# A chain of layers on one core: norm, operands and attention as one stage, the mixture fused with its norms, and PV for two key tiles in one go

## The chip, the cores and the metric

The kernel runs on one core of a Trainium2 chip. The metric is the device time of one execution in microseconds (us). Engines: TensorE (PE: matmuls, PEld: weight loads), VectorE (DVE), ScalarE (ACT), GpSimd (POOL) and SyncE (SP), which here issues nearly all DMAs.

## The reference

On 8 batches of 512 tokens by 128 channels in float32, the reference runs four layers, each an attention part and a feed-forward part, with a norm, a residual and another norm around every part. What the change touches:

- L0 attention: 16 heads of 8 channels. Its heads are a reshape of the token axis and not a split of the channels, so that a head's rows are gathered from many tokens. `softmax(Q K^T) V`, plus x, and a variance over a whole batch.
- L3 attention: 16 heads of 8 channels, rotary embedding on q and k, biases, `softmax(Q K^T / sqrt(8)) V`, output projection.
- L3 feed-forward: an elastic mixture of 4 experts (128 to 512 to 128, ReLU), each weighted per token by a gate value u (a sigmoid) and a rule on u; then the last norm and residual, which is the output.
- The norm: `(x - mean) / sqrt(var + 1e-5)` over 128 channels.

Between them lie channel mix, a test-time learner, a switch layer, linear attention and expert choice, which stay as they are.

## The kernel before

The program is a list of stages (`program`, L2355 on). Each opens a block in which every engine gets its own instruction list; engines meet only by semaphores, and all of them meet at a stage's end. Tokens lie as 32 tiles of 128 tokens by 128 channels; a batch is 4 tiles (`TPB`).

`norms` (L148) is one stage for all 8 batches: VectorE takes statistics (L183, L186), POOL makes scale and shift of a tile (L257 to L260), ScalarE applies them (L344), VectorE adds the residual (L223), TensorE transposes the normalised tiles (L332) and VectorE copies them to `c.nT` (L227). There are nine such stages, norm0 to norm8.

`attention_operands` (L417) is the next stage. For each batch it projects q and k (L486; with rotary also a swapped version, L488) and v (L493), and splits q and k into three bfloat16 parts, so that nine products of bfloat16 rows give a float32-like score: first part on ScalarE (L511), remainder on VectorE (L558), second part on ScalarE (L501), third part on POOL (L601); POOL adds the rotated halves (L590). SP stores the parts in device memory (L462) and loads them in the layout of a quad (L401, L403). VectorE lays v out (L576, L580).

`attention` (L604) runs over 32 quads. A quad is 4 heads' groups of 512 queries and 512 keys. For quad i the kernel needs the maxima of its scores first: 8 max tiles of two matmuls each (L731) into two pairs of banks, reduced by VectorE (L881); POOL splits the maxima in three (L691 to L697), TensorE transposes them (L744), ScalarE copies them (L854), and SP moves them (L662) into the operand rows, so that the score matmul (L750) subtracts the maximum. Then for each of 4 key tiles k there are 4 score matmuls g, an exponential each (L850) and PV for the key tile (L760: 4 column groups of the array, float32). In steady state the maxima of quads i+2 and i+3 are made beside the scores of quad i. TensorE's list, in a loop of four quads, is: score g=0, score g=1, PV of the key tile before, score g=2, a max tile, score g=3, a max tile. Scores have two banks in turn, probabilities two sets. After a quad VectorE copies the output (L890 for L0, L892 for L3). L0 regroups rows on POOL (L409); L3 selects rows by small matmuls (L771). VectorE normalises (L899, L901, L908, L910).

`elastic_mixture` (L2145) prepares the gate's weights for all tokens, loads w1 and w2, and in a second block runs 32 steps (batch by expert): 4 up matmuls (L2208), ReLU (L2242), 16 down matmuls (L2215), and VectorE gathers the weighted result (L2273). The gate's matmuls (L319) are in norm7, the output's store (L362) in norm8.

Of the kernel before, what the change touches and what calls it, by code (L numbers as in the profile page):

```python
# [4 lines left out]
F32 = mybir.dt.float32  # L5
# [367 lines left out]
class Attention:  # L373
# [5 lines left out]
    def __init__(self, c, tag, by_tokens, scale):  # L379
        self.c, self.tag, self.by_tokens, self.scale = c, tag, by_tokens, scale  # L380
        nc = c.nc

        self.q_parts = nc.dram_tensor(f"{tag}_q_parts", (B, PARTS, TPB, HD, 2048), BF16).ap()
        self.k_parts = nc.dram_tensor(f"{tag}_k_parts", (B, PARTS, TPB, HD, 2048), BF16).ap()

        self.q9 = c.take(RING * 1024).bitcast(BF16).rearrange("p (s t) -> p s t", s=RING)
        self.k9 = c.take(RING * 1024).bitcast(BF16).rearrange("p (s t) -> p s t", s=RING)
        if by_tokens:
            self.q_raw = c.take(RING * 1024).rearrange("p (s t) -> p s t", s=RING)
            self.k_raw = c.take(RING * 1024).rearrange("p (s t) -> p s t", s=RING)  # L390
        self.v32 = c.take(2 * 512).rearrange("p (s g k d) -> p s g k d", s=2, g=4, k=4)
        self.qk_in = [c.sem(f"{tag}_qk_in{s}") for s in range(RING)]

        self.v = c.take(QUADS * 128).rearrange("p (q g k d) -> p q g k d", g=4, k=4, d=HD)

    def load(self, sp, b, s):

        q_to, k_to = (self.q_raw.bitcast(BF16), self.k_raw.bitcast(BF16)) if self.by_tokens else (self.q9, self.k9)
        for p in range(PARTS):
            src = self.q_parts[bass.ds(b, 1), p, s].rearrange("o d t -> (o d) t")  # L400
            sp.dma_start(q_to[24 * p:24 * p + 24, s, :],  # L401
                         src.unsqueeze(0).to_broadcast([PARTS, HD, 2048])).then_inc(self.qk_in[s], 16)
            sp.dma_start(k_to[24 * p:24 * p + 24, s, :],  # L403
                         self.k_parts[bass.ds(b, 1), :, s].rearrange("o r d t -> (o r) d t")).then_inc(self.qk_in[s], 16)

    def by_group(self, pool, n, s, signal):

        for raw, rows in ((self.q_raw, self.q9), (self.k_raw, self.k9)):
            pool.tensor_copy(rows[0:QK_ROWS, s, :].bitcast(F32).rearrange("p (g j l) -> p g j l", g=4, j=HEADS),  # L409
                             raw[0:QK_ROWS, s, :].rearrange("p (j g l) -> p g j l", g=4, j=HEADS)).then_inc(signal, 1)  # L410

    def columns(self, rows, g, first, n):

        return rows[:, 512 * g + first:512 * g + first + n]


def attention_operands(c, a, w, tables=None):  # L417

    nc = c.nc
    tag = a.tag + "_op"
    sem = lambda name: c.sem(f"{tag}_{name}")
    q_made, v_made = sem("qk_made"), sem("v_made")
    high, rest, mid, parts, v_laid = (sem(s) for s in ("high", "rest", "mid", "parts", "v_laid"))
    SLOTS = 4
    stored = [sem(f"stored{s}") for s in range(SLOTS)]
    exact = sem("exact")
    LOAD_AT = SLOTS - 1  # L430
    part = c.take(SLOTS * PARTS * 256).bitcast(BF16).rearrange("p (s a t) -> p s a t", s=SLOTS, a=PARTS)
    left = c.take(SLOTS * S).rearrange("p (s t) -> p s t", s=SLOTS)
    if tables is not None:
        full = c.take(SLOTS * S).rearrange("p (s t) -> p s t", s=SLOTS)
        turn = c.take(SLOTS * S).rearrange("p (s t) -> p s t", s=SLOTS)

# [1963 lines left out]
```

## Time and profile before

| | |
|---|---|
| median of 3 runs | 2471.12 us (2436.83, 2471.12, 2471.49) |
| profiled execution | 2424.76 us |
| its span, first to last instruction | 2423.0 us |
| granted TensorE clock, mean | 0.800 |
| busy: PE, DVE, ACT, POOL | 69%, 57%, 46%, 27% |
| instructions | 30093 |

Busy shares are means over stages that differ much. A trace row gives start and length in us, engine, line of the kernel and operation, out<-in with shapes, and in brackets how long the engine had been idle and what ended that. The granted clock is the share of TensorE's full clock.

### The profile page before, as it was taken

To read this page: it belongs to the slowest core of one execution; us is meant where nothing else is said; L and a number is where in the kernel's file an instruction comes from. 1 tells how busy PE (TensorE), PEld (TensorE's weight loads), DVE (VectorE), ACT (ScalarE), POOL (GpSimd) and SP (SyncE) were. 2 spreads that over 40 slices of the span, in tenths; PEclk is the share of its full clock that TensorE was granted. 3 is DMA by queue.
4 is the path that set the end of the run, shared out by engine and by line. 5 is a ranking of instruction groups with operands and counts; after the bars stand their busy time and mean duration, and the time that the engine had idled before them with its cause. 6 is when DMAs were issued, how large, how long until landed. Compare 5 with 4: busy or idle time off the path is not lost. (4 is left out here: it accounts for less than half of the span.)

```text
span 2423.0 us, 30093 instructions
## 1 busy us (share of the span) xinstructions
PE 1679.4 (69%) x8625; PEld 859.8 (35%) x8625; DVE 1376.5 (57%) x3051; ACT 1121.6 (46%) x2093; POOL 651.0 (27%) x1168
## 2 busy tenths in 40 slices
PE   3389999992469952605530185346999999759995
PEld 2212222221346642503430164121333333347774
DVE  4578888865822462034468711646778787453334
ACT  4237777774431241216640031423777777553343
POOL 3222222215510035161051875542000000040002
PEclk9779999995756965756755588576999999959997
DMA  3311111100000003100004022121111111010001
GB/s 80 117 34 50 50 48 48 47 17 0 1 1 1 1 1 101 33 20 1 0 5 135 4 43 26 42 98 42 48 46 44 49 44 46 2 35 0 0 0 35
DMA packets 84907, 84.54 MB, mean 35 GB/s; under 512 B 35927, under 2 KB 67522, under 8 KB 84694
## 3 DMA queue, kind: packets, MB, share of 16 engines
q1 hardware_dynamic: 74902, 76.43, 9.5%
q0 software_dynamic: 7680, 6.06, 1.5%
q10 hardware_dynamic: 2240, 1.05, 0.2%
q8 instruction: 36, 0.59, 0.1%
q14 instruction: 49, 0.40, 0.1%
HBM read 59.78 MB, written 25.17 MB: 35 GB/s over the span
## 5 line engine op out<-in xcount | busy, mean ns | idle before, releaser
L881 DVE TENSOR_REDUCE arena<-psum 128x2 f32<-128x1024 f32 x512 | 603.2, 1219 | 148.6 <-PE psum L731 145.6
L850 ACT ACTIVATE arena<-psum 128x512 f32<-128x512 f32 x1024 | 581.7, 596 | 202.3 <-PE psum L750 180.5
L750 PE MATMUL psum<-arena 99*128 99x512 bf16 x1024 | 390.4, 389 | 20.0 <-ACT arena L850 8.6
L731 PE MATMUL psum<-arena 72*128 72x512 bf16 x1024 | 322.1, 397 | 30.7 <-PEq L448 13.1
L344 ACT ACTIVATE arena<-arena 128x128 f32<-128x128 f32 x512 | 208.4, 481 | 219.9 <-POOL arena L260 194.5
L760 PE MATMUL psum<-arena 128*32 128x512 f32 x2048 | 275.4, 610 | 1.9 <-ACT arena L850 1.9
L332 PE MATMUL psum<-arena 128*128 128x128 f32 x256 | 71.2, 433 | 271.5 <-ACT arena L344 271.5
L750 PEld LDWEIGHTS psum<-arena 99*128 99x128 bf16 x1024 | 98.2, 99 | 403.2 <-ACT arena L850 338.1
L257 POOL TENSOR_SCALAR arena<-arena 128x4 f32<-128x4 f32 x104 | 26.3, 253 | 650.3 <-DVE arena L186 642.7
L691 POOL TENSOR_TENSOR arena<-arena 128x16 bf16<-128x16 f32 x64 | 13.9, 217 | 671.6 <-DVE arena L881 420.1
L183 DVE BATCH_NORM_STATS2 arena<-arena 128x6 f32<-128x128 f32 x512 | 110.3, 278 | 86.9 <-DMA arena<-sw_rows_out,arena 33.7
L2242 ACT ACTIVATE arena<-psum,arena 128x512 f32<-128x512 f32 x128 | 88.1, 689 | 139.9 <-PE psum L2208 139.4
L731 PEld LDWEIGHTS psum<-arena 72*128 72x128 bf16 x1024 | 99.7, 100 | 143.3 <-DVE arena L881 23.5
L332 PEld LDWEIGHTS psum<-arena 128*128 128x128 f32 x256 | 47.5, 223 | 289.4 <-ACT arena L344 289.4
L259 POOL TENSOR_TENSOR arena<-arena 128x4 f32<-128x4 f32 x120 | 128.6, 1072 | 10.4 <-DVE arena L191 1.6
L2215 PEld LDWEIGHTS psum<-arena 128*128 128x128 f32 x1024 | 119.1, 191 | 14.9 <-issue 14.9
L2208 PE MATMUL psum<-arena 128*128 (+1 forms) x256 | 116.6, 599 | 9.8 <-ACTq L2235 9.8
L2273 DVE SCALAR_TENSOR_TENSOR arena<-psum,arena 128x128 f32 (+1 forms) x128 | 36.0, 344 | 152.1 <-PE psum L2215 137.9
L2215 PE MATMUL psum<-arena 128*128 128x128 f32 x1024 | 119.3, 274 | 0.0
L486 PE MATMUL psum<-arena 128*128 128x512 f32 x64 | 44.8, 813 | 79.9 <-DVE arena L558 41.1
L2026 ACT ACTIVATE arena<-psum,arena 128x512 f32<-128x512 f32 x8 | 6.2, 777 | 172.7 <-PE psum L1986 172.7
L1197 ACT ACTIVATE arena<-psum 128x512 f32<-128x512 f32 x48 | 28.7, 598 | 120.7 <-PE psum L1135 63.8
(374 smaller groups left out, 2493.8 us busy)
## 6 DMA issues: line engine op xcount, KB each, us to landing
arena<-L_q_parts SPq DMA_DIRECT2D x192, 96.0 KB
arena<-L_k_parts SPq DMA_DIRECT2D x192, 96.0 KB
L_q_parts<-arena SPq DMA_DIRECT2D x16, 384.0 KB, 3.2
L_k_parts<-arena SPq DMA_DIRECT2D x16, 384.0 KB, 3.2
arena<-in_L_ffn_w SPq DMA_DIRECT2D x1, 2048.0 KB, 10.5
ec_result<-arena SPq DMA_DIRECT2D x1, 2048.0 KB, 9.8
arena<-in_L_ffn_fc2s SPq DMA_DIRECT2D x1, 2048.0 KB, 16.3
ec_normed<-arena SPq DMA_DIRECT2D x1, 2048.0 KB, 8.7
```

The source lines that it names most:

```text
L183: nc.vector.bn_stats(f.stats[:, t, :], src[:, t, :]).then_inc(s_stats, 1)
L259: ch.next(nc.gpsimd.tensor_tensor(f.scale[:, at], f.var_eps[:, at], c.minus_half[:, 0:n], ALU.pow))
L332: last = nc.tensor.transpose(c.bank(b % 2)[:, k * 128:(k + 1) * 128], c.n[:, TPB * b + k, :], c.ident)
L344: nc.scalar.activation(dst[:, t, :], src[:, t, :], ACT.Identity, bias=f.shift[:, t:t + 1], scale=f.scale[:, t:t + 1]).then_inc(signal, 1)
L731: last = nc.tensor.matmul(max_bank[m % 2][:, 512 * h:512 * h + 512], a.columns(q9[0:QK_ROWS, s, :], m // 2, 128 * (2 * (m % 2) + h), 128), ...
L750: nc.tensor.matmul(score_bank[g % 2], a.columns(k9[0:ROWS, s, :], g, 128 * k, 128), a.columns(q9[0:ROWS, s, :], g, 0, 512), start=True, st ...
L760: last = nc.tensor.matmul(out_bank[32 * g:32 * g + 32, :], v32[:, s % 2, g, k, :], prob[:, k % 2, g, :], start=(k == 0), stop=(k == 3))
L850: nc.scalar.activation(prob[:, k % 2, g, :], score_bank[g % 2], ACT.Exp, scale=a.scale).then_inc(probs, 1)
L881: nc.vector.tensor_reduce(neg_max[:, s % 2, col:col + 2], max_bank[m % 2].rearrange("p (h t) -> p h t", h=2), axis=AX.X, op=ALU.max, negat ...
L2208: nc.tensor.matmul(c.bank(k), w1[:, e, 128 * k:128 * k + 128], batch, start=True, stop=True).then_inc(h_made, 1)
L2215: last = nc.tensor.matmul(c.bank(4 + e % 2)[:, 128 * t:128 * t + 128], hT[:, e % 2, k, 128 * t:128 * t + 128], w2[:, e, k, :], start=(k == ...
L2242: nc.scalar.activation(hT[:, e % 2, k, :], c.bank(k), ACT.Relu, bias=b1T[:, CHUNKS * e + k:CHUNKS * e + k + 1]).then_inc(h_done, 1)
```

## The change

It has four parts.

1. **One stage per attention.** `attention_layer` takes the place of norm0, `attention_operands` and `attention` of L0, and of norm6, operands and attention of L3. Before the first quad only batches 0 and 1 are normalised, projected and stored. Batch b+2 is handled beside the four quads of batch b: ScalarE applies the norm tile by tile between exponentials, TensorE transposes and projects behind the max tiles of certain key tiles, ScalarE copies the results out of PSUM, and POOL does all the splitting of operands, the rotary products and the laying out of v (of batches 0 and 1 VectorE splits q). All loops are written out.
2. **One ring of three banks for ScalarE** (banks 4, 5, 7). Scores, row transposes, token transposes and projections take its slots in a fixed order. Maxima and, for L3, the selection use the two pairs of banks in turn as a second ring.
3. **PV for two key tiles in one go, three probability sets.** PV of key tiles 0 and 1 comes after the second score of key tile 2, PV of 2 and 3 after the second score of the next quad's key tile 0.
4. **Mixture fused.** norm7, mixture and norm8 are one stage: the norm, gate and weights of batch b+1 are made beside the steps of batch b, and the last norm and store of batch b-1 too. `project_heads` now follows a barrier of its own.

The diff's core (the rest follows from it: removed are `Attention`, `attention_operands`, `attention`; waits are on constants now):

```
+    def beside(i, k):
+        kind = {(1, 2): "n", (1, 3): "q", (2, 3): "k", (3, 3): "v"}.get((i % TPB, k))
+        b = i // TPB + AHEAD                      # AHEAD = 2
+        return items(b)[kind] if kind and b < B else ()
+    acts = Ring([c.bank(4), c.bank(5), c.bank(7)], for_scalar())
+    maxes = Ring([c.bank(0, 2), c.bank(2, 2)], for_vector())
+    def split_parts(eng, ch, b, n):
+        a, f = part[:, slot_of(b, n), :, :], full[:, n, :]
+        if rope:
+            ch.mark(eng.tensor_tensor(f, f, cos_t, ALU.mult))
+            ch.next(eng.tensor_tensor(other[:, n, :], other[:, n, :], sin_t, ALU.mult))
+            ch.next(eng.tensor_tensor(f, f, other[:, n, :], ALU.add))
+        ch.next(eng.tensor_copy(a[:, 0, :], f))
+        ch.next(eng.tensor_tensor(f, f, a[:, 0, :], ALU.subtract))
+        ch.next(eng.tensor_copy(a[:, 1, :], f))
+        eng.tensor_tensor(a[:, 2, :], f, a[:, 1, :], ALU.subtract).then_inc(part_done[n], 1)
...
+        SP:  for i in range(QUADS):
+                if i < LAST:
+                    max_rows(i + 1)
+                b = i // TPB + AHEAD
+                if i % TPB >= 2 and b < B:
+                    store(b, i % TPB - 2)
+                if by_tokens and i + 5 < QUADS:
+                    load(i + 5)
+                if rope and i + RING < QUADS:
+                    load(i + RING)
...
+        POOL: for i in range(QUADS):
+                r, b = i % TPB, i // TPB + AHEAD
+                if i < LAST:
+                    values(i + 1)
+                if r == 0 and b < B:
+                    of_x.factors(pool, b)
+                if r == 0 and AHEAD < b <= B:
+                    lay_values(b - 1)
+                if rope and r == 1 and b + 1 < B:
+                    of_o.factors(pool, b + 1)
+                if r >= 2 and b < B:
+                    operand(b, r - 2)
+                if by_tokens and i + RING < QUADS:
+                    regroup(i + RING)
+                if i + 2 < QUADS:
+                    split_max(i + 2)
...
+        TensorE, quad i, key tile k:
+                    if k == 0:
+                        pe.wait_ge(max_in[i % RING], 16 * (i // RING + 1))
+                    score_tile(i, k, 0)
+                    score_tile(i, k, 1)
+                    if k == 2:
+                        pv(i, 0)
+                        pv(i, 1)
+                    if k == 0 and i >= 1:
+                        pv(i - 1, 2)
+                        pv(i - 1, 3)
+                    score_tile(i, k, 2)
+                    score_tile(i, k, 3)
+                    if rope and k == 1 and i >= 1:
+                        pick(i - 1)
+                    if i + 2 < QUADS:
+                        if k == 0:
+                            operands_set(i + 2)
+                        max_tile(i + 2, 2 * k)
+                        max_tile(i + 2, 2 * k + 1)
+                    if k == 1 and i < LAST:
+                        turn_max(i + 1)
+                    (batch b: turn_tokens at (1, 2), queries at (1, 3), keys at (2, 3), project_values at (3, 3))
...
+        ScalarE, at = 4 * (i % TPB) + k, after exps(i, k):
+                    if k == 1 and i < LAST:
+                        rows(i + 1)
+                    if b < B and 1 <= at <= 4:
+                        of_x.apply_tile(act, c.n, c.x, TPB * b + at - 1)
+                    if rope and b + 1 < B and 5 <= at <= 8:
+                        of_o.apply_tile(act, c.o, c.o, TPB * b + at - 1)
+                    (copy_tokens at 6, keep q at 7, keep k at 11, keep_values at 15)
...
+        VectorE, quad i, key tile k:
+                    if k == 0 and i >= 1:
+                        out(i - 1)
+                    if k == 1 and i >= 1:
+                        normalise(i - 1)
+                    if i + 2 < QUADS:
+                        take(i + 2, 2 * k)
+                        take(i + 2, 2 * k + 1)
+                    (o_spread at (0, 2), add at (2, 2), x_spread at (3, 2))
...
+        Mixture, TensorE:
+            for g in range(STEPS):
+                b, e = divmod(g, MIX)
+                if g + 1 < STEPS:
+                    up(g + 1)
+                if b + 1 < B and e == 2:
+                    turn(b + 1)
+                if b + 1 < B and e == 3:
+                    gate(b + 1)
+                down(g)
...
-        stage(norms, "norm0", after_layer=False)
...
-        stage(norms, "norm6", after_layer=True, reload=chosen_sums)
-        stage(rotary_attention, d, rotary)
-        stage(norms, "norm7", after_layer=True, gate=mixture.wu)
-        stage(elastic_mixture, d, mixture)
-        stage(norms, "norm8", after_layer=True, x_norm=False, out=out)
+        stage(rotary_attention, d, rotary, chosen_sums)
+        stage(elastic_mixture, d, mixture, out)
```

The lines in words ("SP:", brackets) are for orientation and not in the code.

## Rows read from the trace of the kernel before

**Rows 1.** The page, busy time, share of the span and instructions of each engine.
```profile
PE 1679.4 (69%) x8625; PEld 859.8 (35%) x8625; DVE 1376.5 (57%) x3051; ACT 1121.6 (46%) x2093; POOL 651.0 (27%) x1168
```

**Rows 2.** Stretches: start:end, length, busy of PE, PEld, DVE, ACT, POOL; clock.
```profile
21.70:148.50 126.80, 57.45 (x163) 26.30 (x163) 83.67 (x235) 38.85 (x66) 44.28 (x63) 0.75 0.24 69
129.00:147.00 18.00, 15.48 (x32) 2.28 (x33) 16.63 (x15) 0.27 (x1) 7.15 (x12) 0.50 0.00 1
148.50:552.00 403.50, 390.38 (x2046) 109.43 (x2045) 320.39 (x338) 296.23 (x543) 91.14 (x212) 0.99 0.11 42
214.55:264.49 49.94, 49.24 (x261) 14.04 (x260) 42.18 (x44) 37.16 (x68) 12.50 (x28) 1.00 0.13 48
1519.10:1675.40 156.30, 72.01 (x195) 30.91 (x195) 92.14 (x251) 53.41 (x99) 73.14 (x105) 0.64 0.19 66
1675.40:2100.40 425.00, 413.48 (x2301) 139.16 (x2301) 318.66 (x336) 296.26 (x544) 33.88 (x154) 0.98 0.11 40
1851.67:1904.23 52.56, 51.83 (x293) 17.69 (x292) 42.13 (x45) 37.17 (x68) 4.41 (x20) 1.00 0.12 46
2114.40:2169.80 55.40, 20.89 (x97) 20.07 (x97) 30.68 (x148) 27.99 (x67) 29.76 (x64) 0.53 0.12 38
2169.80:2396.00 226.20, 225.98 (x1280) 163.44 (x1280) 70.76 (x261) 88.14 (x128) 0.00 (x0) 0.99 0.00 0
2396.00:2423.00 27.00, 0.00 (x0) 0.00 (x0) 15.88 (x76) 13.18 (x32) 16.69 (x32) 0.54 0.27 78
```

**Rows 3.** Timeline of one key tile in an L0 quad.
```profile
308.55 2.39 ACT L850 ACTIVATE arena<-psum 128x512 f32<-128x512 f32 x4 [0.66 <-PE psum L750]
309.44 0.81 PE L750 MATMUL psum<-arena 99*128 99x512 bf16 x2
310.18 1.06 PE L760 MATMUL psum<-arena 128*32 128x512 f32 x8
311.18 0.39 PE L750 MATMUL psum<-arena 99*128 99x512 bf16 x1
311.60 2.39 ACT L850 ACTIVATE arena<-psum 128x512 f32<-128x512 f32 x4 [0.66 <-PE psum L750]
312.04 2.36 DVE L881 TENSOR_REDUCE arena<-psum 128x2 f32<-128x1024 f32 x2 [0.51 <-PE psum L731]
```

**Rows 4.** Timeline, selecting matmuls of an L3 quad and the load behind them.
```profile
1856.09 1.08 PEld L771 LDWEIGHTS psum<-arena 128*128 128x128 f32 x8
...
1857.00 0.21 PEld L750 LDWEIGHTS psum<-arena 99*128 99x128 bf16 x2
```

**Rows 5.** Timeline, project_heads: four transposes, four matmuls, the next transposes.
```profile
2108.30 0.60 PE L2089 MATMUL psum<-arena 128*128 128x128 f32 x4
...
2108.74 1.06 PE L2100 MATMUL psum<-arena 128*128 128x128 f32 x8
...
2109.63 0.60 PE L2089 MATMUL psum<-arena 128*128 128x128 f32 x4
```

**Rows 6.** Timeline and DMA issues, pieces of the serial stretches.
```profile
21.74 0.87 DVE L183 BATCH_NORM_STATS2 arena<-arena 128x6 f32<-128x128 f32 x4 [21.74 <-PEq L100]
...
25.10 1.65 ACT L344 ACTIVATE arena<-arena 128x128 f32<-128x128 f32 x4 [3.83 <-POOL arena L260]
...
65.58 0.70 SPq L401 DMA_DIRECT2D arena<-L_q_parts  x1
...
1568.44 0.69 DVE L558 TENSOR_TENSOR arena<-arena 128x512 f32<-128x512 f32 x1
1568.47 1.79 POOL L590 TENSOR_TENSOR arena<-arena 128x512 f32<-128x512 f32 x1 [0.73 <-DVE arena L548]
...
1571.52 1.09 POOL L601 TENSOR_TENSOR arena<-arena 128x512 bf16<-128x512 f32 x1 [1.26 <-ACT arena L501]
...
1572.56 3.47 DVE L568 MEMSET arena<- 32x4096 int32 x1 [0.91 <-issue]
...
1575.04 7.03 ACT L515 ACTIVATE arena<-arena 32x8192 bf16<-32x8192 f32 x1
...
L_q_parts<-arena SPq DMA_DIRECT2D x16, 384.0 KB, 3.2
```

More of the change, by code:

```diff
@@ L370 @@
 RING = 4
[L373 to L414, printed above, removed]
@@ L417, in attention_operands, with __init__, bank, count @@
-def attention_operands(c, a, w, tables=None):
+class Ring:
+    def __init__(self, banks, names):
+        self.banks = banks
+        self.number = {name: n for n, name in enumerate(names)}
+    def bank(self, name):
+        return self.banks[self.number[name] % len(self.banks)]
+    def count(self, name):
+        return self.number[name] + 1
+    def room(self, name):
+        return max(0, self.number[name] + 1 - len(self.banks))
+AHEAD = 2
+def attention_layer(c, tag, w, scale, tables=None, reload=None):
@@ L474, in _, with turn_tokens, project @@
         @block.tensor
         def _(pe):
+            def turn_tokens(b):
+                pe.wait_ge(of_x.normed, TPB * (b + 1))
+                pe.wait_ge(act_taken, acts.room(("n", b)))
+                for k in range(TPB):
+                    last = nc.tensor.transpose(acts.bank(("n", b))[:, 128 * k:128 * k + 128], c.n[:, TPB * b + k, :], c.ident)
+                last.then_inc(act_made, 1)
+            def project(name, weights):
+                b = name[1]
+                pe.wait_ge(act_taken, max(acts.count(("n", b)), acts.room(name)))
+                nc.tensor.matmul(acts.bank(name), weights, c.nT[:, b, 1:S + 1], start=True, stop=True).then_inc(act_made, 1)
@@ new lines, in pv @@
+            def pv(i, k):
+                pe.wait_ge(act_taken, acts.count(("score", i, k, 3)))
+                if k == 0:
+                    pe.wait_ge(v_ready, i + 1)
+                    pe.wait_ge(out_taken, i)
+                for g in range(4):
+                    last = nc.tensor.matmul(out_bank[32 * g:32 * g + 32, :], v32[:, i % 2, g, k, :],
+                                            prob[:, (4 * i + k) % PROBS, g, :], start=(k == 0), stop=(k == 3))
+                last.then_inc(pv_step, 1)
@@ L476, in _, with pick @@
+            def pick(i):
+                pe.wait_ge(out_taken, i + 1)
+                pe.wait_ge(max_taken, maxes.room(("pick", i)))
+                for t in range(4):
+                    last = nc.tensor.matmul(maxes.bank(("pick", i))[:, 36 * t:36 * t + 36], o_quad[:, i % 2, 128 * t:128 * t + 128],
+                                            select, start=True, stop=True)
+                last.then_inc(max_made, 1)
             pe.wait_ge(ordered, 1)
@@ L2150, in elastic_mixture @@
+def elastic_mixture(c, d, small, out):
     nc = c.nc
```

1100 lines of the change are left out of this document (600 added, 500 removed).

## The prediction

> **What bounds the kernel now.** I read the engines' totals first, then the time by stretches, then the order of work inside one quad. The totals [rows 1] name no bound: TensorE 69%, VectorE 57%, ScalarE 46%. The stretches [rows 2] show why. The attention quads run with TensorE recorded as almost always busy, at full clock, VectorE at 84% and ScalarE at 74% (49.94 us for four quads of L0, 12.49 each; 52.56 for four of L3, 13.14 each). Ahead of each attention lies a serial stretch, 126.8 us for L0 and 156.3 us for L3, in which no engine reaches 70% and no exponential runs: norm of all batches, operands of all batches, first maxima. At the end, 55.4 us of norm and preparation lead to the mixture's 226.2 us, which TensorE fills (225.98 busy), and 27.0 us of last norm follow, with TensorE idle.
>
> Inside a quad neither TensorE nor ScalarE is the bound alone: the wait that ends last is a loop [rows 3]. ScalarE does four exponentials in 2.39 us, then idles 0.66. The second of them (end at 308.55 plus 1.20) is the last of a key tile. It frees the bank of a score that starts 0.1 later, PV of the finished tile follows 0.33 behind (310.18) and takes 1.0, the next score starts at 311.18 and reaches ScalarE 0.42 later (311.60). So the loop is 1.20 + 0.43 + 1.0 + 0.42 = 3.05 us per key tile: with two banks and two probability sets, what ScalarE still has in store is shorter than PV and its two handovers. Four of them and the 0.27 us row copy are 12.47, against 12.49 measured. L3 adds the four small selecting matmuls, which hold TensorE 0.91 us [rows 4], of which 0.65 shows.
>
> **The change part by part.** All sums are against the profiled execution, 2424.76 us (span 2423.0).
>
> *Start of L0.* After the change only two batches precede the first quad. Norm of one batch ends 5.0 us after its start (25.10 plus 1.65 less 21.74) [rows 6]; transposing, copying and projecting q at half clock bring the first operand to about +10. VectorE meanwhile has three statistics of 1.25, the pad memset of 3.47 and the ones memset. The ones memset stood on ScalarE at 7.03; VectorE's price for it is unseen: 3.5 if it goes by bytes as the pad memset, 7 if by elements; I take 7. So VectorE starts its operand at +15; four operations of 0.7 with three handovers of 0.16 end at +18. The store is issued and lands 3.2 to 3.7 later, six loads are issued at 0.74 each (0.70 and a gap) and land as much later: +30 [rows 6]. Regrouping takes 2 us, sixteen maxima at 1.18 [rows 3] go to +51, and the first score needs all but the last two: first exponential at about +50 where it is now +126.8. Gain 76.5.
>
> *Start of L3.* Two norms with the residual between give +10.7, four projections at half clock (1.8 each, twice the 0.89 of [rows 5]) and their copies +21. VectorE, with spreads, adds and memsets, is free at +24; seven operations on it take 5.7: +30. Store, loads and maxima as before: first exponential at +60 for 156.3 now. Gain 96. Bound for both starts: 10 us either way each.
>
> *A quad.* I follow the new order from the first score after a PV pair (t=0). Scores 0 and 0.21, two maxima tiles to 1.28, the four scores of the next key tile to 2.6, two maxima tiles, of which the second waits until VectorE, behind the output copy (0.7), has read the earlier one (3.5); the row transpose; scores of the third key tile at 4.09 and 4.3, the latter after the second tile's last exponential; then PV twice, 1.9. The score behind it starts at 6.42 and its exponential at 6.84, though ScalarE had finished at 5.75: 1.1 us idle. The second half is alike, with one exponential fewer in the chain because no transpose takes a bank, but the last maxima tile waits for VectorE until 9.9 and the two scores and the PV pair end at 12.68. So the loop now has 11 exponentials (6.6), two PV pairs (3.8), two pairs of scores (0.86), two round trips (1.04) and 0.4 of VectorE's lateness. The third bank and third set let the first PV of a pair start without a wait, but nothing hides the second one. For L0: 12.68 for 12.49, over 32 quads +6. For L3 the selection moves into VectorE's ring of two banks: the max tile behind it waits until the normalising (0.25, 0.17, 0.29) is done, at about 4.66, so 13.84 for 13.14: +22. Bounds: the engines' own sums. For L0 VectorE has 8x1.18 and 1.5, 11.0; for L3 TensorE has 32 matmuls of 0.213, four PV of 0.95, 0.16 and 0.91, 11.7.
>
> *Side work for six later batches.* TensorE takes four transposes (0.44) and projections (0.89 each) [rows 5]: three for L0 (3.1 us), five for L3 (4.9 us). They stand in TensorE's queue between maxima and scores, so I count them whole. ScalarE's copies behind the second and fourth key tiles fall into its idle time after a PV pair; those behind the first and third (0.41 each) show partly, 0.2. VectorE's statistics behind the maxima delay the output copy by 0.7 (L0), 1.3 with the second norm (L3). Batch sums 3.9 and 6.4; times six: +23.5 and +38. POOL has 16 small copies, operands and regrouping, some 31 us of L0's 50 per batch, in L3 less than 30: nothing waits for it. If that cover goes, each late operand delays a store, and the row transfer behind it on SP. First-quad transpose wait +2, no PV pair in the first quad -1.9, in either layer.
>
> *Mixture.* The norm and residual of batch 0 only, then transposes, copy and gate: first up matmul 14.6 after the start, for 55.4 now. The 226.2 stay; seven further batches add 0.44 and 0.86 each on TensorE, +9. ScalarE and VectorE have room in a batch of 28 us (88.14 and 70.76 busy in 226.2). Behind the last down: 1.2, one norm 5.0, residual 0.7, store 2.7: 9.6 for 27.0. From 308.6 to 259.4: -49.
>
> Sum: L0 -76.5+6+23.5 = -47. L3 -96+22+38 = -36. Mixture -49. One more barrier +1. In all -131: 2294 for the profiled execution.
>
> A side remark on POOL. One of its two-input operations took 1.79 us beside VectorE's two-input operation instead of 1.09 to 1.3 [rows 6]. At the starts, VectorE and POOL split operands at once; at 0.5 for each of some 16 meetings, of which half lie on the path, that is +4, inside the bounds. The Trainium skill (SBUF — State Buffer, Who interferes with whom) says that a VectorE instruction with two inputs in SBUF shares a read port with GpSimd and that one fully blocks. By that rule alone all 16 VectorE operations of 0.69 would be added, 11 us, and the sum would be 2305. The quads are free of it: VectorE's maxima read PSUM.
>
> **The rivals.**
>
> *More is hidden* (0.20). Side work falls into existing waits and the loop is shorter than I traced. For it: ScalarE would still be idle 2.8 of 12.68. Against it: the same method reproduces today's 12.49 to 0.02. The floor is 371 us for L0's quads and 403 for L3's, where I have 435 and 485: 2148; halfway to it, 2220.
>
> *A queue is late* (0.23). SP issues six loads (4.4 us) and, before some, waits for a store; the max-row transfer of the next quad stands behind them. For it: today's row transfers have fewer waits ahead. Against it: the loads are freed about 9 us into a quad, the rows are wanted only 4 us into the next. At 1 us a quad it is 2358, at 2 us 2422, which would be no change.
>
> *The clock* (0.05, slower). With TensorE recorded busy for 15.48 of 18.0 us in the first maxima, the clock was 0.50 [rows 2]; in the quads it is 1.00. That is 1.2 and 2.4 GHz. If PV pairs and waits leave TensorE idle enough for the lower level, a quad costs twice 10.8 instead of 12.68, +9 for L0, and twice 11.7 instead of 13.84, +9.6 for L3. The kernel is slower by over 2% from 19 of the 64 quads on (180 us at 9.3 each); 20 of them give 2480 on the profiled scale. Against it: TensorE's own work per quad is 85% of the time, hardly less than now (87%).
>
> **How the numbers follow.** The forecast case has the remaining 0.52. The three timed runs lie 12, 46 and 47 us above the profiled execution; I add 21, near 1%, for where a median will lie: 2315. The forecast's own range is 2265 to 2355 (starts 10 each, k-ones and port 10, side work 20, offset 20). For 8 in 10 I reach into the first two rivals: 2210 to 2400. A change under 2% is hardly told from none here. Faster by over 2% (profiled time under 2376): the forecast, the first rival and half of the second, 0.83. Within 2%: 0.12. Slower: 0.05.
>
> **What would show it.** First exponentials 50 and 60 us behind the stages' first VectorE instruction (now 126.8 and 156.3); output copies 12.7 and 13.8 apart in late quads and about 1 to 1.6 more in the earlier ones; ScalarE idle about 1.1 us twice a quad, released by TensorE; the mixture's steps 7.0 us as now, and under 12 us behind the last. Wrong would be: quads under 12 us, first scores waiting for the row transfer, POOL named as releaser of scores, or a granted clock under 0.9 in the quads.

## Result: 2328 us for 2457, and where the terms landed

The changed kernel takes 2328.3 us as the median of four runs (2302.2 to 2356.0), the kernel before 2457.5 (four runs). Two of the four runs took 2302 and 2304 us at a mean granted clock of 0.82, two 2353 and 2356 us at 0.80, and the ratio, 0.938 (95% interval 0.923 to 0.952), compares the shorter runs of either kernel: faster, near the forecast of 2315 and inside the range. The profiled execution took 2302.2 us (span 2300.5), where my sum said 2294. The page's totals for the changed kernel, in the columns of [rows 1]:

```profile
PE 1619.6 (70%) x8625; PEld 838.0 (36%) x8625; DVE 1307.5 (57%) x2847; ACT 1072.9 (47%) x2122; POOL 789.8 (34%) x1434
```

As before they name no bound. The stretches do. The changed kernel's, in the columns of [rows 2]: start of L0, its quads, the learner's stage with the norm ahead of it, expert choice, start of L3, its quads, and the fused mixture to the end:

```profile
20.95:83.31 62.36, 26.20 (x67) 8.07 (x68) 38.71 (x52) 8.01 (x18) 27.99 (x46) 0.67 0.20 66
83.30:514.90 431.60, 396.25 (x2142) 123.06 (x2140) 324.33 (x374) 297.60 (x591) 176.56 (x397) 0.99 0.15 51
602.40:822.30 219.90, 163.94 (x801) 111.74 (x802) 95.38 (x332) 70.76 (x147) 29.75 (x64) 0.76 0.00 1
1203.00:1453.20 250.20, 110.16 (x759) 79.67 (x759) 124.37 (x269) 31.16 (x44) 133.08 (x161) 0.67 0.22 50
1477.31:1550.30 72.99, 34.40 (x75) 11.30 (x76) 51.68 (x93) 17.12 (x35) 35.83 (x58) 0.57 0.22 75
1550.30:2022.70 472.40, 439.35 (x2414) 157.95 (x2412) 332.53 (x419) 313.45 (x623) 142.57 (x298) 0.97 0.13 47
2040.89:2300.40 259.51, 238.65 (x1377) 174.98 (x1377) 112.92 (x496) 129.42 (x242) 44.50 (x96) 0.96 0.06 17
```

The kernel before, the two stretches whose code the change leaves alone (same columns):

```profile
638.30:878.90 240.60, 185.57 (x802) 124.48 (x802) 95.72 (x332) 70.80 (x147) 29.77 (x64) 0.68 0.00 1
1259.60:1491.00 231.40, 104.62 (x759) 75.77 (x759) 124.21 (x270) 31.28 (x44) 129.17 (x159) 0.68 0.23 53
```

Set against the forecast, in us ("copies": from the first to the last copy of a quad's output, 31 intervals):

| stretch | before | forecast | after |
|---|---|---|---|
| L0, first VectorE instruction to first exponential | 126.8 | 50 | 62.4 |
| L0 copies | 385.2 | 414.7 | 412.3 |
| L3, the same start | 156.3 | 60 | 73.0 |
| L3 copies | 404.0 | 464 | 454.9 |
| last norm, mixture, last norm | 308.6 | 259.4 | 259.5 |
| learner's stage (code unchanged) | 240.6 | 240.6 | 219.9 |
| expert choice (code unchanged) | 231.4 | 231.4 | 250.2 |

The starts came out 25 us worse than forecast, L3's quads 9 better, and two stages that the change doesn't touch moved by -20.7 and +18.8, which happen to cancel. (Expert choice is counted to VectorE's last instruction here. From its start to the first instruction of the next stage it is 274.3 us for 259.5, +14.8.) The differences in the table sum to -120.7, the spans differ by 122.5.

Half an L0 quad of the changed kernel without side work, as a timeline (start, length; in brackets the idle time before it and what ended it; answers to [rows 3]):

```profile
455.76 1.08 ACT L840 ACTIVATE arena<-psum 128x512 f32<-128x512 f32 x2 [1.25 <-PE psum L734]
455.78 1.03 PE L721 MATMUL psum<-arena 72*128 72x512 bf16 x4
456.64 0.82 PE L734 MATMUL psum<-arena 99*128 99x512 bf16 x3
457.12 2.07 ACT L840 ACTIVATE arena<-psum 128x512 f32<-128x512 f32 x4 [0.28 <-PE psum L734]
457.78 0.39 PE L734 MATMUL psum<-arena 99*128 99x512 bf16 x1 [0.31 <-ACT arena L840]
458.00 0.60 PE L721 MATMUL psum<-arena 72*128 72x512 bf16 x2
458.83 0.60 PE L721 MATMUL psum<-arena 72*128 72x512 bf16 x2 [0.23 <-DVE arena L925]
459.53 0.61 PE L734 MATMUL psum<-arena 99*128 99x512 bf16 x2
460.02 1.08 ACT L840 ACTIVATE arena<-psum 128x512 f32<-128x512 f32 x2
460.07 1.93 PE L744 MATMUL psum<-arena 128*32 128x512 f32 x16
461.93 0.61 PE L734 MATMUL psum<-arena 99*128 99x512 bf16 x2
462.35 1.09 ACT L840 ACTIVATE arena<-psum 128x512 f32<-128x512 f32 x2 [1.25 <-PE psum L734]
```

L734 is the score, L840 the exponential, L721 the maxima, L744 PV. While TensorE does the pair of PVs (460.07 to 461.93), ScalarE runs dry: 1.25 us idle, and as much half a quad before. Four exponentials in a row take 2.07 us when their scores are ready, not the 2.39 of [rows 3], so ScalarE is not what the loop is made of. TensorE stands for others in the key tile behind each pair: 0.31 for a bank that ScalarE has not emptied, 0.23 for maxima that VectorE has not taken. Twice a quad this makes 1.08 us, all that TensorE's record lacks (11.83 busy of 12.91). What I had traced as one loop is two engines that wait for each other in turn.

### The profile page after: what moved, and what is told of

The parts are those of the page before. It is cut to its first block and busy times, and to the rows that moved or that the text cites. A ratio compares the mean times of both kernels' runs of the same rounds, so it can differ in the third digit from the quotient of the medians.

```text
span 2300.5 us, 26232 instructions
## 1 busy us (share of the span) xinstructions
PE 1619.6 (70%) x8625; PEld 838.0 (36%) x8625; DVE 1307.5 (57%) x2847; ACT 1072.9 (47%) x2122; POOL 789.8 (34%) x1434
## 5 line engine op out<-in xcount | busy, mean ns | idle before, releaser
L840 ACT ACTIVATE arena<-psum 128x512 f32<-128x512 f32 x1024 | 540.3, 601 | 213.3 <-PE psum L734 208.5
L734 PE MATMUL psum<-arena 99*128 99x512 bf16 x1024 | 318.5, 390 | 54.2 <-ACT arena L840 36.2
L721 PE MATMUL psum<-arena 72*128 72x512 bf16 x1024 | 301.3, 399 | 58.8 <-DVE arena L925 20.7
L744 PE MATMUL psum<-arena 128*32 128x512 f32 x2048 | 256.7, 619 | 0.2
L734 PEld LDWEIGHTS psum<-arena 99*128 99x128 bf16 x1024 | 84.8, 98 | 308.1 <-ACT arena L840 219.1
L344 ACT ACTIVATE arena<-arena 128x128 f32<-128x128 f32 x320 | 129.4, 481 | 127.0 <-POOL arena L260 101.6
L332 PE MATMUL psum<-arena 128*128 128x128 f32 x160 | 44.5, 433 | 172.9 <-ACT arena L344 172.9
L721 PEld LDWEIGHTS psum<-arena 72*128 72x128 bf16 x1024 | 88.2, 99 | 209.0 <-DVE arena L925 80.1
L623 POOL COPY arena<-arena 72x1024 f32<-72x1024 f32 x64 | 65.0, 1042 | 180.9 <-PE psum L734 157.7
L2330 PEld LDWEIGHTS psum<-arena 128*128 128x128 f32 x1024 | 118.1, 192 | 8.2 <-issue 8.2
L2330 PE MATMUL psum<-arena 128*128 128x128 f32 x1024 | 119.9, 275 | 0.0
L257 POOL TENSOR_SCALAR arena<-arena 128x4 f32<-128x4 f32 x56 | 14.2, 254 | 303.2 <-DVE arena L186 299.2
L2318 PE MATMUL psum<-arena 128*128 128x512 f32 x256 | 116.9, 600 | 0.0
L2451 DVE SCALAR_TENSOR_TENSOR arena<-psum,arena 128x128 f32<-128x128 f32 x128 | 36.0, 344 | 127.1 <-PE psum L2330 126.4
L744 PEld LDWEIGHTS psum<-arena 128*32 128x32 f32 x2048 | 54.2, 111 | 136.2 <-issue 89.9
L332 PEld LDWEIGHTS psum<-arena 128*128 128x128 f32 x160 | 29.7, 224 | 183.7 <-ACT arena L344 183.7
L2253 ACT ACTIVATE arena<-arena 128x128 f32<-128x128 f32 x124 | 50.3, 481 | 92.7 <-POOL arena L2241 92.7
```

What stands on the lines that cost most here:

```text
L332: last = nc.tensor.transpose(c.bank(b % 2)[:, k * 128:(k + 1) * 128], c.n[:, TPB * b + k, :], c.ident)
L344: nc.scalar.activation(dst[:, t, :], src[:, t, :], ACT.Identity, bias=f.shift[:, t:t + 1], scale=f.scale[:, t:t + 1]).then_inc(signal, 1)
L623: nc.gpsimd.tensor_copy(rows[0:QK_ROWS, i % RING, :].rearrange("p (g j l) -> p g j l", g=4, j=HEADS), raw[0:QK_ROWS, i % RAW, :].rearrange ...
L721: last = nc.tensor.matmul(bank[:, 512 * h:512 * h + 512], columns(q9[0:QK_ROWS], i, m // 2, 128 * (2 * (m % 2) + h), 128), columns(k9[0:QK ...
L734: nc.tensor.matmul(acts.bank(name), columns(k9[0:ROWS], i, g, 128 * k, 128), columns(q9[0:ROWS], i, g, 0, 512), start=True, stop=True).the ...
L744: last = nc.tensor.matmul(out_bank[32 * g:32 * g + 32, :], v32[:, i % 2, g, k, :], prob[:, (4 * i + k) % PROBS, g, :], start=(k == 0), sto ...
```

## Experiments

All spans of stretches below are from one profiled execution each.

**The fused mixture alone** on the kernel before: its last three stages replaced by

```
-        stage(norms, "norm7", after_layer=True, gate=mixture.wu)
-        stage(elastic_mixture, d, mixture)
-        stage(norms, "norm8", after_layer=True, x_norm=False, out=out)
+        stage(elastic_mixture, d, mixture, out)
```

> Edit: the kernel before with the changed kernel's mixture alone (LayerNorm inside it, steps unrolled, output stored batch by batch); norms, operands and attention stay as separate stages. By the prediction's term the tail from the last attention stage on goes from 308.6 to 259.4 us, so the whole is 49 us shorter than before: a ratio of 0.980. Rival A: the first start of the mixture depends on what the attention stage leaves (queues, banks), so that the gain differs from the changed kernel's own 259.6 us by more than 2 us. Rival B: part of the 49 us was a gain of the joint stage, and the ratio is 0.987 or above (under 32 us). The mixture's 32 steps should stand 7.0 us apart.

Ratio to before 0.980 (0.971 to 0.989). From the last output copy of L3 to the end: 325.0 us before, 276.9 here, 277.8 in the changed kernel. So -48.1 of the forecast -49, by itself, within 1 us of the changed kernel: by this stretch both rivals fall. The whole can't decide: its interval reaches past the 0.987 at which rival B begins, and the profiled span is only 3.3 us shorter than before, because two stages of unchanged code took longer, the learner's 271.2 us for 240.6 and expert choice some 14 more. Four steps of the mixture, one batch, take 29.4 us for 28.0, the 1.3 of the batch's own transposes and gate on TensorE.

**PV for one key tile at a time**, on the changed kernel:

```
-                    if k == 2:
-                        pv(i, 0)
-                        pv(i, 1)
+                    if k >= 1:
+                        pv(i, k - 1)
                     if k == 0 and i >= 1:
-                        pv(i - 1, 2)
                         pv(i - 1, 3)
```

> Edit: the changed kernel with PV for one key tile at a time (after the scores 0 and 1 of the next key tile), three probability sets kept. Theory: the quad is TensorE's own list plus two short waits per key tile (for the fourth score's bank and for the second half of the maxima); each lone PV of 0.93 us stands between the scores, so ScalarE has a stall of about 0.4 us in each key tile instead of 1.25 us in every second, and the sum of TensorE's list is unchanged: late quads of layer 0 within 0.2 us of the changed kernel's 12.91, those of layer 3 within 0.2 of 13.75, whole within 10 us. Rival A (the diff's second half is what costs: two PV in a row drain the score ring): late quads 12.5 in layer 0, near the kernel before's 12.49, the whole 20 to 25 us shorter. Rival B (two PV at once save a wait each): 13.3 or more, the whole 20 us longer.

Late quads: 11.63 us in L0, 12.86 in L3. My theory fell, and rival A was too timid: the copies span 375.9 us in L0 and 423.7 in L3, 36.4 and 31.3 less than the changed kernel. Three windows: a late quad of the changed kernel,

```profile
455.47:468.38 12.91, 11.83 (x66) 3.48 (x65) 10.41 (x11) 8.75 (x17) 3.18 (x8) 1.00 0.04 16
```

and, with PV split, a late quad and 100 us of earlier ones:

```profile
424.00:435.63 11.63, 11.63 (x73) 3.44 (x65) 10.36 (x12) 8.97 (x19) 3.21 (x7) 1.00 0.04 14
350.00:450.00 100.00, 100.00 (x561) 30.92 (x563) 87.45 (x95) 76.94 (x148) 35.55 (x82) 1.00 0.14 48
```

In L0 TensorE's record has no pause left. Its timeline with PV split shows why: ScalarE's pauses are short and even, and TensorE has no wait in brackets:

```profile
431.73 0.60 PE L734 MATMUL psum<-arena 99*128 99x512 bf16 x2
432.21 1.09 ACT L837 ACTIVATE arena<-psum 128x512 f32<-128x512 f32 x2 [0.28 <-PE psum L734]
432.26 1.06 PE L744 MATMUL psum<-arena 128*32 128x512 f32 x8
433.26 0.61 PE L734 MATMUL psum<-arena 99*128 99x512 bf16 x2
433.69 1.09 ACT L837 ACTIVATE arena<-psum 128x512 f32<-128x512 f32 x2 [0.39 <-PE psum L734]
433.71 1.03 PE L721 MATMUL psum<-arena 72*128 72x512 bf16 x4
```

So PV in pairs, part 3 of the change, costs 68 us in the two layers. Some 8 of L3's 31 are a matter of the clock. Five of the changed kernel's 31 intervals between L3's copies are 1.6 us longer than their like. In each, about 5 us behind the copy, the granted clock fell to 0.5 (1.2 GHz) for 3.4 us and a PV pair took 3.1 to 3.6 us for 1.92. One such stretch with its clock, its pair, and the same pair of a quad earlier:

```profile
1618.50:1621.90 3.40, 3.40 (x18) 0.60 (x16) 1.40 (x2) 1.38 (x4) 0.00 (x0) 0.50 0.05 14
1618.80 3.46 PE L744 MATMUL psum<-arena 128*32 128x512 f32 x16
1604.06 1.92 PE L744 MATMUL psum<-arena 128*32 128x512 f32 x16
```

Ahead of each fall TensorE had stood for the bank and the maxima (0.31 and 0.23 us). The two other profiles with the changed kernel's quads show five such falls each, those with interleaved maxima and without side work one each. The kernel before and all seven kernels with PV split show none between L3's copies. Why these five of 31, and none in L0, stays open.

Yet the whole (median 2283.6, ratio 0.938) was only 8 us shorter in the profiled execution: the learner's stage, same code, took 282.7 us for 219.9. More on that below.

**Maxima interleaved**, on the changed kernel: scores 0, 1, (PV), 2, maxima a, score 3, maxima b.

> Edit: the changed kernel with TensorE's order in a key tile changed from scores 0, 1, 2, 3, maxima a, b to scores 0, 1, 2, maxima a, score 3, maxima b. Theory (TensorE's list with its two short waits sets the quad): the first maxima fill the wait of 0.31 to 0.5 us for score 3's bank, and VectorE begins on them earlier, so that the second wait (0.23 to 0.39) shrinks too: late quads of layer 0 12.0 to 12.3 us instead of 12.91, layer 3 12.9 to 13.2 instead of 13.75; 62 quads by 0.6 to 0.9 make 35 to 55 us less in all. Rival A (the loop through ScalarE's exponentials sets it): score 3 comes 0.3 to 0.4 us later to ScalarE in every key tile, and quads are 13.0 to 13.6, the whole 10 to 40 us longer. Rival B (VectorE's two reductions per key tile set it): no change, quads within 0.1 us of 12.91.

Late quads 12.47 and 13.16; copies 399.2 and 432.0 us, 13 and 23 less. The direction is the theory's, the size half of it in L0: the wait for the bank went, the one for the maxima stayed, at 0.30 twice a quad. The whole (median 2327.6 us, ratio 0.957, 0.950 to 0.964) would have misled: its profiled execution took 2327.3 us, 25 more than the changed kernel's, and again the learner's stage took 282.6.

**The first row of maxima ahead of the loads of quad 3**:

```
             load(2)
-            load(3)
             max_rows(0)
+            load(3)
```

> Edit: at the start of each attention stage of the changed kernel the transfer of the first quad's row of maxima is issued on SyncE's queue before the loads of quad 3 instead of behind them. Theory: that 12 KB transfer landed 8 to 10.5 us after its issue since it stood behind the loads of quads 2 and 3; with one of them behind it, it lands in 4 to 7 us, and the first exponential is 3 to 6 us earlier in each layer, 6 to 12 us in all. Rival A: a row transfer takes as long in any place (a scattered write), no change within 2 us. Rival B: SyncE waits for the row's own source and holds the loads of quad 3 back, so that quad 3's operands are late: first exponential earlier but the third or fourth quad longer by as much, the sum unchanged.

L3's start in the changed kernel, with the row's transfer (SPq L549) and the first score and exponential:

```profile
1538.69 0.74 SPq L549 DMA_DIRECT2D arena<-arena  x1
1549.65 1.91 PE L734 MATMUL psum<-arena 99*128 99x512 bf16 x4 [6.82 <-DMA arena<-arena]
1550.29 2.07 ACT L840 ACTIVATE arena<-psum 128x512 f32<-128x512 f32 x4 [10.33 <-PE psum L734]
```

and with the row first:

```profile
1542.13 0.74 SPq L549 DMA_DIRECT2D arena<-arena  x1
1546.07 1.93 PE L734 MATMUL psum<-arena 99*128 99x512 bf16 x4
```

11.0 us from issue to score become 3.9. The theory holds for L3: the first exponential comes 65.7 us after the stage's first VectorE instruction, 71.7 to 73.7 in seven profiles with the row behind the loads. L0 shows rival B: the first exponential is 4.6 us earlier (78.72 for 83.31), the first copy 3.7 later (106.24 for 102.57), for TensorE's transpose for quad 1 then waits for POOL, which waits for quad 3's late operands, regroups them (2.0 us) and lays out values (5.5 us) ahead of splitting quad 1's maxima:

```profile
94.41 0.30 PE L728 MATMUL psum<-arena 128*48 128x128 bf16 x1 [9.28 <-POOLq L636]
```

The Trainium skill (DMA: Bandwidth & Descriptors, Queues, rings and completion order) says that a queue's descriptors on one DMA engine are consumed in ring order. These runs agree: from the issue of a 12 KB transfer to the score that needs it are 11.0 us, or 3.9 and perhaps less for the landing, by what stands ahead of it.

**No side work in the quads**: norm, projections and operands of batches 2 to 7 left out, and those of the first two read again.

> Edit: the changed kernel without the work of the later batches inside the quads (norm, transposes, projections, operands, stores of batches 2 to 7; for L3 of batches 2 to 7 as well); the quads of the later batches read the operands of the first two again. It leaves that part of the computation out. Theory of the prediction: the side work cost 3.9 us (layer 0) and 6.4 us (layer 3) for each of six batches, and nothing else slows the early quads: all quads of layer 0 at the late quads' 12.91 us, of layer 3 at 13.75; from first to last output copy 412.3 becomes 395 us in layer 0 (six times 2.87 less), 454.9 becomes 418 in layer 3 (six times 6.2 less). Rival A: late quads are short since the loads have ended too, so that quads without side work but with loads are 13.2 or more. Rival B: the POOL's share of the side work only stands at an idle place, and early quads stay within 0.3 us of what they were.

Up to the last two, which have no maxima beside them, every quad of L0 is 12.91 (copies 395.1 us) and every one of L3 13.75 (421.3), but for one of 15.44 in which the clock fell. So side work costs 17.2 us in L0, 2.87 for each of six batches. In L3 33.6 us went with it, but four falls of the clock, some 6.6 us, are part of that, which leaves 27, 4.5 a batch. The loads are hidden, as the theory has it.

**Two banks in ScalarE's ring**, with PV split: `acts = Ring([c.bank(4), c.bank(5)], for_scalar())`.

> Edit: PV for one key tile at a time, as in the run with PV split (late quads 11.63 and 12.86 us), and ScalarE's ring of two banks in place of three. Theory: with three banks and lone PVs TensorE was busy without a pause (100.00 us of 100); with two banks the third score waits for the first exponential in each key tile, some 0.2 to 0.4 us, four times a quad: late quads of layer 0 12.3 to 12.9 us, near the kernel before's 12.49, which had two score banks and lone PVs as well. Rival A: TensorE's list hides these waits, quads within 0.1 us of 11.63, and the third bank is worth nothing. Rival B: transposes, side projections and the scores share two banks now, and early quads rise by over 1.5 us while late ones don't.

Late quads 11.98 and 13.21, 0.35 more only; quads with side work 13.5 to 14.2 in L0 where they had been 12.5. Copies 403.9 and 451.0: the third bank is worth 28 and 27 us, nearly all of it where side projections share the ring. Rival B in kind, not the theory: of its 1.5 us for early quads, 0.9 to 1.7 came for three in four and 0.4 for the fourth.

**Two probability sets**, with PV split: `PROBS = 2`.

> Edit: PV for one key tile at a time and two probability sets in place of three. Theory: a lone PV of key tile k-1 ends before the exponentials of k+1 begin, so that two sets do: quads within 0.1 us of 11.63 in layer 0 and 12.86 in layer 3. Rival: the exponentials of k+1 wait for the PV of k-1, which stands behind two scores, and the quad is 0.4 to 1.2 us longer (up to 12.8).

Copies 375.9 and 423.6, late quads 11.63 and 12.86: no difference at all. The third set buys only the pairing, which costs.

**The best version**: PV split, in L3 alone the row first, and

```
-            nc.vector.memset(k9[MAX_ROW:128, :, :], 1.0).then_inc(k_ones, 1)
+            nc.vector.memset(k_words[MAX_ROW:128, :, :].rearrange("p s t -> p (s t)").bitcast(I32), 0x3F803F80).then_inc(k_ones, 1)
```

> Edit: the changed kernel with PV for one key tile at a time; in layer 3 the first row of maxima issued before the loads of quad 3; and the ones of the key operands written as 32-bit words (half as many elements). Theory: against the changed kernel's profiled run 36 us less in layer 0's quads, 31 in layer 3's (as in the run with PV split), 7.5 at layer 3's start, 3.4 at each start from the ones, some 81 us in all if the stages between, whose code is the same, take what they took there (2220 us); with the learner's stage at the lower granted clock, as in the run with PV split (283 instead of 220 us), 2210 to 2285. Ratio to the kernel before 0.91 to 0.935. Rival A: the ones are hidden behind the loads, and both starts stay (7 us more). Rival B: the learner's stage is at the lower clock in all runs of this kernel, because layer 0's quads leave TensorE no pause: no run below 2265. Rival C: it comes and goes from run to run whatever stands before it: the runs fall into groups 20 to 60 us apart, the lowest below 2240.

Median 2254.9 us (2238.7 to 2263.6, six runs); ratio to before 0.933 (0.922 to 0.943). The ones take 3.47 us for 6.88. L0's first exponential comes 59.4 us after the stage's first VectorE instruction, 62.4 to 62.9 in the seven profiles without these ones and without the row first. L3's comes after 65.1, for 65.7 with the row first alone, and after 63.6 to 64.7 in three later profiles: there the ones give 2 us at most, so that rival A is partly right. Copies 376.0 and 423.7. The learner's stage took 266.6 us. All six runs lie within 25 us, below rival B's 2265 and in no two groups as rival C has it. Against the changed kernel's first profile the span is 48 us shorter: the stretches that were edited gave some 78, the learner's stage took 47 back, and expert choice, code unchanged, gave 15. The Trainium skill (VectorE: DVE Perf Modes, Zero memsets can be issued as uint32) says that a memset takes one cycle per element whatever the type: the 6.88 and 3.47 agree, and here for a value other than zero.

**The changed kernel again**, beside the next three:

> The changed kernel once more, beside the next three, to have its stages of unchanged code against theirs. Theory (the granted clock of the learner's stage differs from run to run whatever stands before it): layer 0 412.3 and layer 3 454.9 us from first to last output copy, as in its first profile, and the learner's stage anywhere between 220 and 283 us. Rival (the joint stage with its pauses leaves the learner a higher clock): the learner's stage within 5 us of 220 again and its fast runs at 2295 to 2305.

Copies 412.2 and 454.9; learner's stage 222.2 us; runs 2287.9 to 2290.6, and one of 2362.9; ratio 0.940 (0.931 to 0.949). The rival's 220 within 5, the shorter runs 5 to 7 us below its 2295. The run of 2362.9, at a granted clock of 0.79 for 0.82, was not profiled, so that the theory doesn't fall either. Expert choice took 231.1 us, for 250.2 in this kernel's first profile.

**Idle time before the learner**, on the best version: a stage of nine VectorE memsets after its norm, between 605.5 and 644.1 us.

> Edit: the best kernel so far (PV split, layer 3's row first, 32-bit ones) with a stage of nine VectorE memsets, some 38 us in which TensorE does nothing, put in before the learner's stage. It took 2252.6 us with the learner's stage at 266.6 us, where the changed kernel's took 219.9. Theory (the clock there does not hang on a pause before it): 38 us longer, 2277 to 2300, learner's stage 255 to 283 us as before. Rival (TensorE's full use in layer 0 is what lowers the clock there, and idle time gives it back): the learner's stage falls to 220 to 240, and the whole is no more than 10 us longer, below 2265.

The profiled span is 2242.1, 10 us shorter than the best version's 2252.6 in spite of 40 us in which TensorE does nothing. From the end of the stage before to the learner's end, with the idle time in it:

```profile
562.00:821.30 259.30, 163.28 (x801) 111.02 (x802) 126.62 (x341) 70.76 (x147) 29.74 (x64) 0.72 0.00 1
```

and in the best version:

```profile
563.00:829.60 266.60, 210.65 (x802) 139.82 (x802) 96.05 (x332) 70.76 (x147) 29.75 (x64) 0.61 0.00 1
```

Less the 40 it is 219. The rival, not the theory, for two of the four runs (2243.9, 2246.0); the other two took 2310.4 and 2318.9, with a lower clock over the whole run. So it is no improvement to ship: the median is 2278.2.

**Interleaved maxima on the best version**:

> Edit: the best kernel so far with TensorE's order scores 0, 1, PV, 2, maxima a, score 3, maxima b. Theory: TensorE has no pause left in layer 0's quads (100.00 us busy of 100), so that no order of its list can be shorter: late quads 11.63 us in layer 0, 12.86 in layer 3, as without it; quads with side work may be 0.1 to 0.5 us shorter. Rival: the fourth score comes later to ScalarE, whose exponentials then hold TensorE up: late quads 11.9 to 12.4 us.

L0: copies 376.3, late quads 11.63, as the theory says of a TensorE without pauses. L3: 12.64 for 12.86, copies 417.2 for 423.7; the selecting matmuls leave a pause there that this fills. Profiled 2248.9 us; one run, so by its stretches and not by its time it is the best attention of all.

**Row first and POOL's order changed**, on the best version: the split of quad 1's maxima ahead of `regroup(3)` and `lay_values(1)`.

> Edit: the best kernel so far, with the first row of maxima issued before the loads of quad 3 in layer 0 too, and on POOL the split of quad 1's maxima before the regrouping of quad 3 and the layout of batch 1's values (in the run with the row first alone, TensorE's transpose for quad 1 waited 9.28 us for POOL, which stood at the regrouping of quad 3). Theory: the first exponential 4.6 us earlier as there, and the first output copy, which had come 3.7 us later, now 3 to 6 us earlier than 99.5, at 93.5 to 96.5 us; the rest as in the best kernel. Rival A: quad 3's operands become late instead, and the fourth quad is longer by what the first gained: no change in the fourth copy's time. Rival B: POOL's next split (quad 2's) waits behind the regrouping, and nothing is gained.

A miss: first exponential at 75.66 (80.51 in the best version), first copy at 102.57, for 99.49; the whole, 2269.7 us and a ratio of 0.931 (0.926 to 0.937), is not told apart from the best version's. The wait moved once more. On POOL the factors of batch 2's norm now stand behind the regrouping, and ScalarE's queue holds the norm's first tile ahead of the exponentials of the third key tile:

```profile
92.43 0.49 ACT L2244 ACTIVATE arena<-arena 128x128 f32<-128x128 f32 x1 [8.38 <-POOL arena L2239]
92.83 2.04 ACT L838 ACTIVATE arena<-psum 128x512 f32<-128x512 f32 x4
93.46 0.61 PE L735 MATMUL psum<-arena 99*128 99x512 bf16 x1 [7.86 <-ACT arena L838]
```

## Why the prediction was right, and where it was not

**Start of L0** (forecast 50, measured 62.4) and **of L3** (60, 73.0): mechanism right, size off by 12 and 13. The term that failed is the row transfer, which I had priced inside the chain from maxima to scores as if nothing stood ahead of it: the run with the row first shows 7 us of it in L3, 5 in L0. That is what showed in the place of a free transfer, and it is one of the signs that I had named as wrong, first scores waiting for the row transfer. Most of the rest, 5 us in either layer, had come when the first operands were there (35.1 us after L0's first instruction for +30, 46.8 after L3's for +42, that is L3's +30 with L0's 12 for store and loads): six loads and the store took longer to land beside each other than the 3.2 of [rows 6], and in L0 POOL waited 9.87 us for them. I had called this rival "a queue is late" and placed it in the quads, where loads are hidden (no side work: 12.91 throughout); it sat at the starts.

**The ones memset** at 7: measured 6.88, by elements. **A quad**: L0 12.68 forecast, 12.91 measured; L3 13.84 and 13.75. The number was good and its account was not. I summed a loop through 11 exponentials of 0.6; four take 2.07 us. What stands in its place is the PV pair, which the split run prices at 1.28 us a quad in L0, 1.08 of it the recorded waits, and 0.89 in L3. The pauses named (ScalarE 1.1 twice a quad: 1.25) and "nothing hides the second one" were right. And the view from it was too narrow: my floor of 11.0 for a quad was VectorE's, while TensorE's list without a pause is 11.63.

**Side work** 3.9 and 6.4 a batch: measured 2.87 and, without the falls of the clock, some 4.5. I counted TensorE's part whole and more on top. Of the 61 us forecast 17 did not come, the "more is hidden" rival in small; that they fell into TensorE's waits is argued, not shown.

**The shared port** was to cost 4. In L0 two of eight VectorE operations beside POOL's grew, 0.43 to 0.71 and 0.69 to 1.46, 1.0 us in all, and in L3 five, by 3.6 us, the longest of them the third row here:

```profile
42.31 0.71 DVE L513 CAST arena<-arena 128x512 bf16<-128x512 f32 x1
43.06 1.46 DVE L514 TENSOR_TENSOR arena<-arena 128x512 bf16<-128x512 f32 x1
1515.88 1.64 DVE L514 TENSOR_TENSOR arena<-arena 128x512 bf16<-128x512 f32 x1
```

The sum, 4.7 us for seven operations, is near the 4, but most of it fell on batch 1: ahead of L3's first operands stand 1.2 us of it. The 11 us for 16 operations added whole did not come, for fewer met.

**Mixture** -49: -49.1 in the changed kernel; from L3's last copy on, where the mixture alone gave -48.1, it is -47.2. It is the most exact term: from the last down matmul to the end 9.6 us for 9.6, and a batch of steps longer by 1.3, as forecast.

**The clock** in the quads is 0.99 and 0.97. Yet the rival came in small: five of L3's quads ran at 0.89 or 0.90, where I had named a clock under 0.9 as a sign of being wrong, and cost some 8 us in all. It goes with paired PV, as the rival has it. In L3's 454.9 us it does not stand out, because the side work there had been priced 11 us too high. A far larger swing came where nobody had changed anything, see below. That the profiled execution came within 8 us of the sum owes something to luck: -20.7 and +18.8 in the unchanged stages, 25 too little at the starts, 12 too much in the quads.

## What to carry to other kernels

Two short pieces of work for one engine, put back to back to save handovers, leave the engine that feeds on the others without input for the whole pair; when it comes back, the first engine waits for it. Spread them, one behind each unit of the feeder's work, and look for the order in which the fullest engine's record has no bracket. Before a small transfer is priced, write down what stands ahead of it in its queue. And compare kernels stretch by stretch: two orders that gained 68 and 36 us in the attention gained 8 and lost 25 in the whole, through a stage that neither had touched.

## What was not expected of the hardware

The learner's stage with its norm, the same code in all kernels, took 219.9, 222.2 and 222.2 us after the attention with paired PV (the third with the row first), 240.6 in the kernel before and 271.2 in the same kernel with the new mixture, whose code is identical up to there, 266.6 to 294.3 in six kernels with PV split, 282.6 with interleaved maxima, 275.4 without side work. The granted clock goes with it: over the stage 0.76 at 219.9 us, 0.68 at 240.6, 0.56 at 282.7. 20 us in the middle of the stage, in the changed kernel,

```profile
722.40:742.40 20.00, 18.54 (x114) 13.09 (x112) 9.15 (x26) 5.93 (x11) 0.00 (x0) 1.00 0.01 2
```

and with PV split:

```profile
664.90:684.90 20.00, 19.23 (x63) 13.06 (x62) 5.80 (x15) 2.85 (x6) 0.00 (x0) 0.50 0.00 0
```

At 1.2 instead of 2.4 GHz TensorE does 63 matmuls instead of 114, and its record is busy for over 90% either way. What decides between the levels stays open. Idle time ahead of the stage went with the higher level in two of four runs, in the profiled one by its clock, in the other by its time. But the four profiles at 219 to 222 are also those in which the stage before had ended at 602 to 606 us or (with the idle time) the learner was put off by 40, so that its place in time is not told apart from the idle time; the kernel before and its twin, 31 us apart at the same place, show that chance has a part. The mean clocks of all runs, profiled or not, hint at more than chance: a mean granted clock of 0.818 or more came in 8 of 12 runs with paired PV, side work and the maxima as in the changed kernel, in 2 of 4 with the idle time, and in none of 19 with PV split (0.796 to 0.811) nor of 4 with the maxima interleaved on the changed kernel. That is a correlation, and no experiment here parts what TensorE did in L0 from when L0 ended.

Expert choice took 249 to 250 us in five profiles and 231 in all others, at the same clock (0.67 and 0.68). Four of the five are the first four experiments, made on one chip; the eight later ones, at 231, were made on two others. So the chip may be what differs, and where two whole times come from different chips this difference can be in them.
